# A gated cross-attention and top-8 router block: router products moved behind the output projection, fewer VectorE steps from logits to mix, gate joined to the experts' table, new slots

## The reference, cut to what matters

```python
x = x + tanh(g_xattn) * xattn(layernorm(x), ctx, mask)   # in patches of 128 positions, 8 heads of 32
x = x + tanh(g_ffn) * ffn(layernorm(x))

# xattn: q, k = Wq z + bq, Wk z + bk;  v = Wv ctx + bv;  softmax(q k / sqrt(32));  gelu(attn v);  Wo o + bo;  * mask
# ffn:
logits = flat @ router_weight.T + router_bias            # (4096 channels, 64 experts)
scores = softmax(logits)
topk_w, topk_idx = top_k(scores, 8)
w_sum = topk_w.sum(-1)
out = flat * w_sum + w_dense @ expert_bias               # w_dense: the 8 weights in place, 0 elsewhere
```

## Time and profile before

| | |
|---|---|
| median of 3 runs | 1337.79 us (1337.01 to 1338.66) |
| the profiled execution | 1338.8 us, of which its span is 1336.7 us |
| TensorE busy (page) | 1281.4 us, 96% |
| VectorE busy | 999.8 us, 75% |
| ScalarE busy | 896.1 us, 67% |
| GpSimd busy | 715.0 us, 53% |
| granted TensorE clock | 0.996 of full |
| DMA | 116.17 MB, mean 87 GB/s |

### The profile page before, as it was taken

The page is one execution under the profiler, slowest core; times in us unless marked ns, Lnnn a source line. Parts: engine busy times, 40 slices in busy tenths (PEclk is TensorE's granted clock), DMA queues, the critical chain, the costliest instruction groups (busy, mean ns, idle before and its releaser), DMA issues.

```text
span 1336.7 us, 38004 instructions
## 1 busy us (share of the span) xinstructions
PE 1281.4 (96%) x15371; PEld 1135.2 (85%) x15371; DVE 999.8 (75%) x1888; ACT 896.1 (67%) x1592; POOL 715.0 (53%) x663
## 2 busy tenths in 40 slices
PE   2899999999999999999999999999999999999986
PEld 2898898888888899798888889888888889979875
DVE  6567768797678966888678876879767896686666
ACT  2466776766686777766667677676668677776654
POOL 2466655456655665456663665545665566545520
PEclk9999999999999999999999999999999999999999
DMA  8331111631117111451114411163112711141003
GB/s 265 97 105 50 34 38 42 206 109 35 40 57 258 34 39 41 131 184 42 34 41 163 151 35 38 42 207 108 37 39 69 246 34 40 40 130 58 26 5 126
DMA packets 120621, 116.17 MB, mean 87 GB/s; under 512 B 11392, under 2 KB 88320, under 8 KB 120320
## 3 DMA queue, kind: packets, MB, share of 16 engines
q1 hardware_dynamic: 119584, 113.74, 27.6%
q10 hardware_dynamic: 864, 0.01, 0.0%
HBM read 80.06 MB, written 33.65 MB: 85 GB/s over the span
## 4 chain that ended last, share of the span: by engine, by line
PE 89%; ACT 4%; DVE 3%; DMA 1%; issue 1%; POOL 1%; SPq 1%; ACTq 0%; DVEq 0%; POOLq 0%
PE ring L281 10%; PE ring L282 9%; PE ring L283 9%; PE ring L398 5%; PE ring L366 5%; PE ring L400 5%; PE ring L399 5%; PE ring L357 4%; PE ring L297 4%; PE ring L296 4%; PE ring L298 4%; PE ring L320 4%; PE ring L380 4%; PE ring L413 4%; PE PR L425 3%; PE ring L462 2%
## 5 line engine op out<-in xcount | busy, mean ns | idle before, releaser
L281 PE MATMUL ring<-z_hi,wqk_hi 128*128 128x256 f32 x1024 | 298.1, 291 | 27.5 <-DVE z_lo L937 23.7
L1018 POOL TENSOR_TENSOR cx_lo<-cx,cx_hi 128x512 fp32r<-128x512 f32 x128 | 165.4, 1292 | 257.8 <-ACT cx_hi L602 257.8
L282 PE MATMUL ring<-z_hi,wqk_lo 128*128 128x256 f32 x1024 | 291.3, 285 | 0.0
L283 PE MATMUL ring<-z_lo,wqk_hi 128*128 128x256 f32 x1024 | 291.1, 284 | 0.0
L281 PEld LDWEIGHTS ring<-z_hi,wqk_hi 128*128 128x128 f32 x1024 | 197.8, 193 | 39.9 <-issue 39.9
L783 DVE SCALAR_TENSOR_TENSOR xt<-ring,cst,mg 128x256 f32<-128x256 f32 x256 | 112.1, 479 | 143.4 <-PE ring L400 143.4
L767 DVE RECIPROCAL o<-ring 128x512 f32<-128x512 f32 x64 | 214.1, 3346 | 1.1 <-PE ring L366 1.1
L1012 POOL TENSOR_TENSOR z_lo<-z,z_hi 128x1024 fp32r<-128x1024 f32 x63 | 151.6, 2406 | 117.6 <-ACT z_hi L586 117.6
L282 PEld LDWEIGHTS ring<-z_hi,wqk_lo 128*128 128x128 f32 x1024 | 198.2, 194 | 0.0
L283 PEld LDWEIGHTS ring<-z_lo,wqk_hi 128*128 128x128 f32 x1024 | 198.1, 193 | 0.0
L1024 POOL TENSOR_TENSOR X<-X,xt 128x512 f32<-128x512 f32 x128 | 163.5, 1280 | 48.7 <-DVE xt L783 38.5
(11 more groups left out here) (134 smaller groups left out, 3035.0 us busy)
## 6 DMA issues: line engine op xcount, KB each, us to landing
cx<-in_ctx SPq DMA_DIRECT2D x128, 256.0 KB, 2.7
out_y<-X SPq DMA_DIRECT2D x128, 256.0 KB, 3.0
X<-in_x SPq DMA_DIRECT2D x112, 256.0 KB, 5.4
mg<-in_mask SPq DMA_DIRECT2D x64, 128.0 KB, 3.2
X<-in_x SPq DMA_DIRECT2D x8, 512.0 KB, 8.3
sel<-rows_d SPq DMA_DIRECT2D x256, 3.0 KB
X<-in_eb SPq DMA_DIRECT2D x2, 512.0 KB, 8.2
X<-in_wqT SPq DMA_DIRECT2D x1, 512.0 KB, 11.3
```

What stands on the lines that cost most here:

```text
L281: e.matmul(o, wqk_hi[:, t, cols], z_hi[:, t, :], t == 0, False)
L282: e.matmul(o, wqk_lo[:, t, cols], z_hi[:, t, :], False, False)
L283: last = e.matmul(o, wqk_hi[:, t, cols], z_lo[:, t, :], False, t == DT - 1)
L1018: e.tensor_tensor(cx_lo[:], cx[p % NC][:], f32(cx_hi[:]), ALU.subtract).then_inc(cxlo_g, 1)
```

## The change

In words:

- The slots are new. On TensorE `R` (49.75 to 47.5) now stands behind `WO` and in front of `S`; `LT` in front of `DEN`; `wT` (43 to 41) behind `hT` and in front of the second `v`; `ST` directly behind that `v` and in front of all `mix`. The other orders of TensorE stay. On ScalarE `ot_hi` goes in front of `v_ev` of the first patch, `wt_hi` in front of `ht_hi`, and the second `v_ev` of the batch's unit behind the first `sx`. On VectorE and GpSimd `norm2` (25.25 to 29.25) goes behind `ht_lo` and behind `ot_lo`; `bn1` comes 1.75 slots later. Which bank each group gets, and so which reader it waits for, follows anew.
- `c_base` (VectorE, slot 34.5) is new: it multiplies `dm` by the reciprocal deviation, makes `gate` = deviation's reciprocal times tanh of the gate, and writes `lr` = `swb` * `dm` + router bias, for the four channel tiles. It stands behind `xt` and in front of `top`. `c_top` then needs one loop of four from `LT` to the logits in place of two.
- `c_weights`: the reciprocal goes first; the weights `w2` come out of one multiplication of 128x512 in place of four of 128x128; the sum and the rest of the scale's steps go behind it, one step fewer.
- The gate's tanh is multiplied into the experts' table `eb2` once, at the start (ScalarE's copy has a scale, VectorE's subtraction is a multiply and subtract), and no longer into the weights.

```diff
--- before.py
+++ after.py
@@ -41,20 +41,20 @@
 
 SLOTS = dict(
 
-    rows=-11.75, z32=-25.75, z_hi=-17, z_lo=-17.5, q=-11, q_ev=-12, k=-9, k_ev=-6.5,
-
-    c_hi=-13.25, c_lo=-10.5, v=-10, v_ev=-6.75, v_gap=-5,
-
-    S=0, top=2.75, split=5.75, MT=7.5, mt_ev=9, ST=13.5, exp=16.25, DEN=18.25, PV=20.75, rc=19, on=21,
-
-    gelu=24, mg=5, ot_hi=25.5, ot_lo=29.25, WO=30, WO_gap=1.5, xt=32, x1=35.25, bn2=39.5,
-
-    h=35.75, hT=39.75, hT_gap=0.25, ht_hi=42.25, ht_lo=44.25, R=49.75,
-
-    norm2=25.25, L=33.5, LT=35.25, c_top=35.75, c_exp=39.25, c_w=41.25, wT=43, wt_hi=43.5, wt_lo=42.5, mix=44.5, m_gap=0.25,
-    sx=44.75, sx_gap=1.5, x2=46.5, rl=54.75, rl_gap=1,
-
-    x_1=0.5, x_gap=3.75, bn1=66.75, bn1_gap=1.75, norm1=96.75,
+    rows=-11.75, z32=-25.25, z_hi=-17.5, z_lo=-17, q=-10, q_ev=-11, k=-9, k_ev=-6.5,
+
+    c_hi=-13.25, c_lo=-10, v=-9.5, v_ev=-6.25, v_gap=-4.25,
+
+    S=1, top=2.75, split=5.75, MT=7.25, mt_ev=8.25, ST=10.5, exp=16, DEN=19.75, PV=20.75, rc=19, on=21,
+
+    gelu=24, mg=5, ot_hi=25.5, ot_lo=27.75, WO=30, WO_gap=1.5, xt=31.75, x1=35.25, bn2=39.5,
+
+    h=35.75, hT=39.75, hT_gap=0.25, ht_hi=43.75, ht_lo=43.25, R=47.5,
+
+    norm2=29.25, c_base=34.5, L=33.25, LT=35.25, c_top=36.25, c_exp=39.25, c_w=41.25, wT=41, wt_hi=43.5, wt_lo=42.5, mix=44.5, m_gap=0.25,
+    sx=44.75, sx_gap=1.5, x2=46.25, rl=55.75, rl_gap=1,
+
+    x_1=0.5, x_gap=3.75, bn1=68.5, bn1_gap=1.75, norm1=97,
 )
 
 
@@ -138,13 +138,14 @@
         lg = sb("lg", [128, DT, NX])
         lr = sb("lr", [128, DT, NX])
         ex = sb("ex", [128, DT, NX])
-        w2 = sb("w2", [128, DT, 2 * NX])
+        w2 = sb("w2", [128, DT, 2, NX])
         t8 = sb("t8", [128, DT, 8])
         sc = sb("sc", [128, DT, 8])
         wt_hi = sb("wt_hi", [128, DT, 128], F32R)
         wt_lo = sb("wt_lo", [128, DT, 128], F32R)
         onef = sb("onef", [128, 128])
         half = sb("half", [128, DT])
+        gate = sb("gate", [128, DT])
 
         ring = [pb(f"ring{i}") for i in range(NR)]
         PR = pb("PR")
@@ -186,8 +187,8 @@
         gelu_a, othi_a, otlo_g, wo_pe, xt_v, x1_g = (sem(n) for n in ("gelu", "othi", "otlo", "WO", "xt", "x1"))
         bn2_v, agg2_v, neg2_v, rstd2_g, h_a, ht_pe, hthi_a, htlo_v, r_pe = (sem(n) for n in (
             "bn2", "agg2", "neg2", "rstd2", "h", "hT", "hthi", "htlo", "R"))
-        l_a, lt_pe, dm_v, lg_v, t8_v, neg_v, mr_v, sel_v, ex_a, w2_v, ac_v = (sem(n) for n in (
-            "L", "LT", "dm", "lg", "t8", "neg", "mr", "sel", "ex", "w2", "ac"))
+        l_a, lt_pe, dm_v, base_v, lg_v, t8_v, neg_v, mr_v, sel_v, ex_a, w2_v, ac_v = (sem(n) for n in (
+            "L", "LT", "dm", "base", "lg", "t8", "neg", "mr", "sel", "ex", "w2", "ac"))
         wm_v, wT_pe, wthi_a, wtlo_v, mix_pe, sx_a, x2_v = (sem(n) for n in (
             "wm", "wT", "wthi", "wtlo", "mix", "sx", "x2"))
 
@@ -249,7 +250,7 @@
                 for u in due(t, C["hT"] + C["hT_gap"] * a):
                     take(("hT", 2 * u + a), t, C["ht_lo"] - C["hT"], htlo_v, 2 * u + a + 1)
             for b in batch(t, C["LT"]):
-                take(("LT", b), t, C["c_top"] - C["LT"], dm_v, 2 * b + 2)
+                take(("LT", b), t, C["c_top"] - C["LT"], lg_v, b + 1)
             for b in batch(t, C["wT"]):
                 take(("wT", b), t, C["wt_lo"] - C["wT"], wtlo_v, b + 1)
             for i in range(16):
@@ -442,9 +443,9 @@
                     e.wait_ge(freed, k)
                 if b == NB - 1:
                     keep_on(bank("wT", b)[:], 20)
-                e.wait_ge(w2_v, 4 * (b + 1))
-                for t in range(DT):
-                    last = e.transpose(bank("wT", b)[:, t * 128:(t + 1) * 128], w2[:, t, :], ident[:])
+                e.wait_ge(w2_v, b + 1)
+                for t in range(DT):
+                    last = e.transpose(bank("wT", b)[:, t * 128:(t + 1) * 128], w2[:, t, :, :].rearrange("p a x -> p (a x)"), ident[:])
                 last.then_inc(wT_pe, 1)
 
             def mix(b, t, c):
@@ -695,7 +696,7 @@
                     e.wait_ge(sm_wr, 16)
                     e.activation(wr2[:, :, 0:NX], wrst, ACT.Copy).then_inc(a_w, 1)
                     e.wait_ge(sm_eb, 32)
-                    e.activation(eb2[:], ebst, ACT.Copy).then_inc(a_w, 1)
+                    e.activation(eb2[:], ebst, ACT.Copy, scale=cst[:, TF:TF + 1]).then_inc(a_w, 1)
                 for u in due(t, C["z_hi"]):
                     z_high(u)
                 for u in due(t, C["q_ev"]):
@@ -810,20 +811,26 @@
                 e.wait_ge(hthi_a, n + 1)
                 e.tensor_tensor(ht_lo[a][:], bank("hT", n)[:], f32(ht_hi[a][:]), ALU.subtract).then_inc(htlo_v, 1)
 
-            def c_top(b):
+            def c_base(b):
                 if b == 0:
                     e.wait_ge(sm_rb, 16)
-                e.wait_ge(dm_v, 2 * b + 1)
+                    e.wait_ge(sm_small, 96)
+                e.wait_ge(dm_v, 3 * b + 1)
+                e.wait_ge(rstd2_g, b + 1)
+                e.tensor_tensor(dm[:], dm[:], ln2[:, 2, :], ALU.mult).then_inc(dm_v, 1)
+                e.tensor_scalar(gate[:], ln2[:, 2, :], cst[:, TF:TF + 1], None, ALU.mult).then_inc(dm_v, 1)
+                e.wait_ge(dm_v, 3 * b + 2)
+                for t in range(DT):
+                    last = e.scalar_tensor_tensor(out=lr[:, t, :], in0=swb[:], scalar=dm[:, t:t + 1], in1=rbb[:],
+                                                  op0=ALU.mult, op1=ALU.add)
+                last.then_inc(base_v, 1)
+
+            def c_top(b):
+                e.wait_ge(base_v, b + 1)
                 e.wait_ge(lt_pe, b + 1)
                 for t in range(DT):
-                    last = e.scalar_tensor_tensor(out=lr[:, t, :], in0=swb[:], scalar=dm[:, t:t + 1],
-                                                  in1=bank("LT", b)[:, t * NX:(t + 1) * NX], op0=ALU.mult, op1=ALU.add)
-                last.then_inc(dm_v, 1)
-                e.wait_ge(dm_v, 2 * b + 2)
-                e.wait_ge(rstd2_g, b + 1)
-                for t in range(DT):
-                    last = e.scalar_tensor_tensor(out=lg[:, t, :], in0=lr[:, t, :], scalar=ln2[:, 2, t:t + 1], in1=rbb[:],
-                                                  op0=ALU.mult, op1=ALU.add)
+                    last = e.scalar_tensor_tensor(out=lg[:, t, :], in0=bank("LT", b)[:, t * NX:(t + 1) * NX],
+                                                  scalar=ln2[:, 2, t:t + 1], in1=lr[:, t, :], op0=ALU.mult, op1=ALU.add)
                 last.then_inc(lg_v, 1)
                 e.wait_ge(lg_v, b + 1)
                 for t in range(DT):
@@ -841,23 +848,21 @@
 
             def c_weights(b):
                 e.wait_ge(ex_a, b + 1)
+                e.reciprocal(sc[:, :, 3:4], sc[:, :, 1:2]).then_inc(wm_v, 1)
                 e.wait_ge(sel_v, b + 1)
                 e.tensor_tensor(ex[:], ex[:], lr[:], ALU.mult).then_inc(wm_v, 1)
-                e.reciprocal(sc[:, :, 3:4], sc[:, :, 1:2]).then_inc(wm_v, 1)
-                e.wait_ge(wm_v, 6 * b + 2)
-                e.tensor_reduce(sc[:, :, 2:3], ex[:], AX.X, ALU.add).then_inc(wm_v, 1)
-                e.tensor_scalar(sc[:, :, 4:5], sc[:, :, 3:4], cst[:, TF:TF + 1], None, ALU.mult).then_inc(wm_v, 1)
                 if b:
                     e.wait_ge(wT_pe, b)
-                e.wait_ge(wm_v, 6 * b + 4)
-                for t in range(DT):
-                    e.tensor_scalar(w2[:, t, :].rearrange("p (a x) -> p a x", a=2),
-                                    ex[:, t, :].unsqueeze(1).to_broadcast([128, 2, NX]),
-                                    sc[:, t, 4:5], None, ALU.mult).then_inc(w2_v, 1)
-                e.tensor_tensor(sc[:, :, 5:6], sc[:, :, 2:3], sc[:, :, 4:5], ALU.mult).then_inc(wm_v, 1)
-                e.wait_ge(wm_v, 6 * b + 5)
-                e.tensor_tensor(sc[:, :, 5:6], sc[:, :, 5:6], ln2[:, 2, :].unsqueeze(2), ALU.mult).then_inc(wm_v, 1)
-                e.wait_ge(wm_v, 6 * b + 6)
+                e.wait_ge(wm_v, 5 * b + 2)
+                e.tensor_tensor(w2[:], ex[:].unsqueeze(2).to_broadcast([128, DT, 2, NX]),
+                                sc[:, :, 3:4].unsqueeze(3).to_broadcast([128, DT, 2, NX]), ALU.mult).then_inc(w2_v, 1)
+                e.tensor_reduce(sc[:, :, 2:3], ex[:], AX.X, ALU.add).then_inc(wm_v, 1)
+                e.wait_ge(wm_v, 5 * b + 3)
+                e.tensor_tensor(sc[:, :, 5:6], sc[:, :, 2:3], sc[:, :, 3:4], ALU.mult).then_inc(wm_v, 1)
+                e.wait_ge(wm_v, 5 * b + 4)
+                e.wait_ge(dm_v, 3 * b + 3)
+                e.tensor_tensor(sc[:, :, 5:6], sc[:, :, 5:6], gate[:].unsqueeze(2), ALU.mult).then_inc(wm_v, 1)
+                e.wait_ge(wm_v, 5 * b + 5)
                 e.tensor_scalar(sc[:, :, 6:7], sc[:, :, 5:6], 1.0, None, ALU.add)
                 e.tensor_tensor(sc[:, :, 7:8], sc[:, :, 5:6], ln2[:, 0, :].unsqueeze(2), ALU.mult).then_inc(ac_v, 1)
 
@@ -892,7 +897,7 @@
                 if b:
                     e.wait_ge(rstd1_g, b)
                 if b >= 2:
-                    e.wait_ge(dm_v, 2 * (b - 1))
```

(6 more changed lines are left out.)

## The result

The changed kernel takes 1357.73 us (median of 4 runs, 1355.51 to 1358.01) against 1337.4 for the kernel before on the same chip: 1.0145 times, 95% interval 1.0133 to 1.0158. The forecast was 1327, its range ended at 1334, and 0.08 stood on slower. The profiled span goes from 1336.7 to 1353.6 us. That is 16.9 us where the medians are 20.3 apart: the profiled execution of the changed kernel is the quickest of its four (1355.51 us at a mean granted clock of 0.994; the others took 1357.65 to 1358.01 at 0.989 to 0.990).

What follows compares the result with a forecast made beforehand. TensorE was taken as the bound: only its own time, its waits and the two ends count. Terms −10.5 + 0.7 − 1.4 = −11.2 us took the median from 1337.79 to 1327 us; range 1315 to 1334.

Steps and rivals of the forecast that it cites:

- slower: Whole kernel: a result slower than the 1335.1 to 1340.5 us counted as the same; chance 0.08.
- Part 1: Router products on TensorE, moved behind the output projection: 0.19 us saved per unit, −10.5 us in sum.
- cover: Scores 0.94 us later after the projection: costed at nothing in plain units; without cover up to 0.94 us per unit.
- Part 2: The batch of 8 units, with its reordered router and weights work: +0.1 us per batch, +0.7 us in sum.
- the collision: VectorE's `c_base` ahead of the maxima, beside GpSimd's additions to X on shared ports: one in the way, about 1.1 us.
- The second collision that I weighed: VectorE's `not_equal` in the batch, 0.9 us earlier, falls on GpSimd's `cx_lo` of 1.30 us.
- Point (d): Batch's mix on TensorE: a bank waits for ScalarE's first exp, so mix ends at most about 1.2 us earlier.
- the bubble goes whole: TensorE's batch wait for `wt_lo` vanishes fully: 7 × 1.6 = 11 us below forecast, 1315 to 1316; chance 0.08.
- Part 3: End of the run, the last batch with nothing beside it: logits and weights end earlier, −1.4 us in sum.
- The second term: End of the run, from the logits' end to the weights' end: 0.85 us earlier.
- The slower one: VectorE before the turned maxima: `c_base`, then `not_equal`, blocked; 3 us lost in each of 7 batches, 1347 us; chance 0.07.
- the two delays overlap: VectorE in the batch: delays at `c_base` and `not_equal` don't add, either covers the other; about 1.1 us taken.

Runs made afterwards that it cites:

- e11: Kernel before, code untouched, with router products behind the value product except each batch's last unit's, which keep their old place: 1328.6 us, 0.9930 times before.
- e1: Kernel before with only R's slot changed (49.75 to 47.5), router products behind the projection and before the scores: 1366.28 us, 1.0215 times before.
- e2: Changed kernel with R put back between scores and denominators (47.5 to 50.25): 1357.64 us, 1.0144 times before.
- e3: Changed kernel with `c_base` behind the reciprocal instead of ahead of the maxima (34.5 to 35.5): 1349.71 us, 1.0088 times before.
- e5: e3 with the negation of the maximum moved from VectorE to ScalarE: 1341.6 us, 1.0025 times before.
- e10: e9 with the negation of the maximum on ScalarE: 1325.35 us, 0.9904 times before.
- e9: Changed kernel with R behind the value product except each batch's last unit's, kept early; `c_base` and logits ahead of scaling and split: 1325.43 us, 0.9908 times before.
- e7: Changed kernel's code with the slots of the kernel before, `c_base` between reciprocal and split: 1339.9 us, 1.0010 times before.

## Why the prediction was wrong

**Part 1, right in its rows.** The 0.19 us per unit, the 0.12 behind the projection and the 1.21 from scores to denominators are all as forecast, and e11 gets 10 us from them.

**Part 1, wrong in its cover.** "So I cost it at nothing there": this step failed. I followed the 0.94 us of later scores to the gelu, to `ot_lo` and to the next projection, and that holds in the changed kernel (the projection waits for `ot_lo` 3.3 us in 2 places, as before). I didn't follow them to the maxima and the split, which slid onto `cx_lo` of GpSimd, nor to the keys' eviction behind them. The price is 19.50 − 18.13 = 1.37 us in one unit of each batch, 7 × 1.37 = 9.6 us, nearly all that the move brings. Alone, in the old code, the move costs more, 28 us (e1): there the units of 19.65 and 19.86 are long as well. Of this, e2 shows that it comes with R's place; that the caught split is all of the 1.37 is likely by the rows (0.99 of it is the cast's length), but no run took the lock alone out of that unit.

**Part 2, the collision was mis-sized.** The sum put one GpSimd operation, 1.1 us, in `c_base`'s way, and its widest bound put two, both additions to X. It is three, with `cx_lo`: the maxima are 4.48 − 1.48 = 3.0 us late. `c_base` doesn't wait once as a block: each new step can be caught by the next GpSimd operation, and GpSimd ran three of them without a pause (865.25 to 868.99). The prediction also took its case from operations with two inputs in SBUF; `gate`, the casts and the negation have one tensor input and were caught all the same. The second collision that I weighed, at `not_equal`, didn't occur: it took 0.42 us (877.81), as before. The stretched unit so came to 33.17 instead of 30.3, 7 × 2.87 = 20.1 us. e3 and e5 take 2.25 of it off again, by two edits that only move small operations from beside GpSimd's. Two things weren't in the prediction at all: the bank that q waits for (1.03 us, covered by the wait for the split as shown above), and the clock behind the 1.94 us wait (0.2 us where it fell).

**Point (d), wrong in the changed kernel.** ScalarE, by exp, was to set the batch's end, since "ScalarE has no pause". It has one there: it waits 1.50 us for the negation and up to 1.02 for `wT`. And exp isn't what ends the batch: the next scores stand 12.67 to 12.77 us behind the first mix product wherever exp is. In e5's batch of the table it is 12.68 too, with exp at 24.54. The forecast's 30.3 less 12.68 asks for the first mix product at 17.6 us, and it came at 20.17 to 20.55, because the split did. With most collisions gone, exp can be seen to count: in e10 and in two batches of e9 the first mix product is at 17.73 to 18.04, and a stretched unit of 29.74 has exp at 25.13, one of 30.00 at 25.38. There (d) fits. In e9's batch of the table the stretched unit and the one behind it take 48.75 us together, against 48.72 before and 48.44 forecast, and 48.07 in the two batches where L871 isn't caught, 48.31 in e10. So the forecast's size was about right once the locks are out, and the rival "the bubble goes whole" found no support: mix no longer waits for `wt_lo`, and at most 0.65 us per batch is gained in the middle of the run.

**Part 3, mis-sized on the good side.** −2.4 us instead of −1.4: from the last scores to the end of the logits 39.1 us (before 40.8), from there to the end of the weights 3.71 (before 4.53). The second term was forecast at 0.85 and is 0.82; the first was forecast at 0.5 and is 1.68. A candidate for what is over is the 1.14 us of the router products that no longer stand behind the last scores: part 1 charged their new place (0.94) and nothing gave back the old one. The runs don't agree on it. With R put back (e2) the way to the logits is 1.5 us longer than in the changed kernel, 40.6; but with R alone moved (e1) it is 40.6 too, only 0.2 below before; and in e7, with R at its old place, it is 38.4. So the cause of this extra 1.2 us stays open. VectorE, end of the changed kernel, to be set beside the earlier trace rows:

```profile
1331.51 0.86 DVE L832 SCALAR_TENSOR_TENSOR lg<-ring,ln,lr 128x64 f32<-128x64 f32 x4
...
1335.39 0.69 DVE L857 TENSOR_TENSOR w<-ex,sc 128x512 f32<-128x512 f32 x1
```

**The sum.** 9.6 + 20.1 − 1.0 = 28.7 us above the forecast's span of 1325.7: 1354.4, against 1353.6 measured. The medians of measurement and forecast are 30.7 apart; 2 us of this are the profiled execution's, the quickest of its four.

**The rivals.** The slower one named the place, `c_base` ahead of the maxima, and 3 us per batch, which is what the maxima lost, and gave 1347. With the crowded unit's 9.6 it would have been 1356.6. That its number fits is partly luck: it was made of both additions (2.7) and `not_equal` (1.3), less a cover of 0.5; the second didn't come about, and `cx_lo` in front of the maxima, which it didn't have, did. I gave it 0.07 because "the two delays overlap"; that argument spoke of the pair `c_base` and `not_equal`, and not of the delays within `c_base`. The start's row had shown the lock plainly, and the batch's cast of 16 columns at 0.69 us had shown that even a tiny operation is caught.
